# Transposed tokens of a mixture layer, laid out token by token

## The chip, the cores and the metric

One core of one Trainium2 chip runs the whole kernel. The metric is the device time of one execution in microseconds, lower is better. TensorE, VectorE, ScalarE, GpSimd and SyncE run their own instruction streams and meet at semaphores.

## What is computed

A decoder layer on 16 batches of 256 tokens by 256 numbers, in float32. Three residual blocks follow each other: a Fourier attention, a cross attention with 16 heads, and a feed-forward block of two mixture layers ("up" and "down") with 64 experts, of which each token takes two. Only the third touches the change:

```python
def kmoe(x_flat, W_router, A, B, scale, bias, d_in1, d_in2, d_out1, d_out2, top_k):
    logits = x_flat @ W_router.T
    vals, idx = jax.lax.top_k(logits, top_k)
    probs = jax.nn.softmax(vals, axis=-1)
    xs = x_flat.reshape(-1, d_in1, d_in2)
    Ag = A[idx]
    Bg = B[idx]
    Y = jnp.einsum('nkoi,nij,nkpj->nkop', Ag, xs, Bg)
    out = jnp.einsum('nkop,nk->nop', Y, probs).reshape(-1, d_out1 * d_out2)
    return out * scale + bias
x_flat = x.reshape(-1, D1 * D2)          # 64 rows of 1024 for each batch
h = kmoe(x_flat, W_up, A_up, B_up, ..., 32, 32, 64, 64, 2)
h = jax.nn.gelu(h, approximate=False)
y = kmoe(h, W_down, A_down, B_down, ..., 64, 64, 32, 32, 2)
```

A mixture token is four rows of 256, so a batch has 64 of them (`TOKENS`), each a 32 by 32 matrix.

## The kernel before

All weights lie in SBUF from the start, the activations of a batch too, and eight PSUM banks are shared by turns. The work of a batch is cut into named steps. A table of words, `ORDER`, fixes by hand in which order the steps are issued, and `step.2@1` means part 2 of the step for the batch one turn back. Every engine walks through the same table and issues those steps that it has code for, so four neighbouring batches are in flight at once and no engine ever takes its steps out of this order. A second table, `DRAIN`, orders what is left of the last two batches.

The third layer norm leaves its rows in `xn3` (128 rows by 2 by 256). The steps that then use the tensor of the change, `xn3T`, are these:

- `ln3_turn` (TensorE, L871): four transposes put `xn3` into the PSUM bank `F`, 512 columns, ordered by column half `c`, token `n` and row `r` within the token.
- `ln3_keep` (ScalarE, L674): one copy of 128 partitions by 512 numbers from `F` to `xn3T`. Before, `xn3T` is `[128, 8, 64]`: for each of the eight pairs of row `r` and half `c` the 64 tokens lie side by side.
- `logits_up` (TensorE, L882): eight matmuls, each with the 64 tokens of one `(r, c)` as the stationary operand (the weights that are loaded) and 64 columns of the router matrix `r_up` as the moving one. [...]
- `own_act` (ScalarE, L683) and `own_dve` (VectorE, L1121): eight copies each of 32 partitions by 256 numbers, from `xn3T` to `own`. Both run through `own_parts` (L362 to L367). `own` holds every token's matrix once for each of its two experts. A copy writes every fourth number there, in 32 groups (`v`, `p`) of eight (`a`), and reads for `a` a number from another of the eight rows of `xn3T`.
- `up` (TensorE, L935 and L941): the matmuls of the experts. The first part needs all of `own`, and the experts' matrices in `chosen_up`. Of those SyncE brings half by DMA (`choose_sync`, L478), 32 transfers for parts 0 to 3 and 32 for parts 4 to 7, the latter as the slots of parts 0 to 3 come free.

Around `own_dve` the table has this order, in which VectorE walks: `mask.3@1`, `own_dve@2`, `y_keep.2@3` (L1234), `catch_b.2@1` (L1087), `dn_weigh.3@3` (L1224, writes `W_dn`), `scale.3@1` (L1098), `y_keep.3@3`. On TensorE `dn_second.3@3` (L974) needs `W_dn`, and `y_turn@3` (L987) needs `y_keep.3`. Only after both does TensorE come to `up.0@2`. Around `logits_up` TensorE has `score.0@1` (L810, L813), `logits_up@2`, `q.2@1`, `q.3@1` (L797), `turn1` (L745) and `turn_a.0@1` (L820), and the last of these needs the scaled probabilities of VectorE's `scale.0@1` (L1098).

Of the kernel before, what the change touches and what calls it, by code (L numbers as in the profile page):

```python
# [16 lines left out]
P = 128  # L17
BATCH, SEQ, DIM = 16, 256, 256
RT = SEQ // P
CT = DIM // P  # L20
HEADS, KEY = 16, 64
PAIRS = HEADS // 2
EXPERTS, TOPK = 64, 2
TOKENS = SEQ * DIM // 1024
D1, F1 = 32, 64
UP_TOK = P // D1
# [23 lines left out]
def at(b, per_batch, k):  # L50

    return b * per_batch + k


def after(eng, sem, value):

    if value > 0:
        eng.wait_ge(sem, value)
# [133 lines left out]
def decoder_layer(nc, t, out):  # L192
    ctx = ExitStack()
    with ctx:
        def sb(name, shape, dt=F32):
            return ctx.enter_context(nc.sbuf_tensor(name, shape, dt))
# [26 lines left out]
        r_up = sb("r_up", [P, 2 * UP_TOK, EXPERTS])  # L223
# [13 lines left out]
        xn = sb("xn", [P, RT, DIM])  # L237
        xnT = sb("xnT", [P, CT, SEQ])
        xn3 = sb("xn3", [P, RT, DIM])
        xn3T = sb("xn3T", [P, 4 * CT, TOKENS])  # L240
        stats = sb("stats", [P, 3, RT, 6])
        moments = sb("moments", [P, 3, RT, 2])
        var_eps = sb("var_eps", [P, 3, RT])
# [20 lines left out]
        h = sb("h", [P, UP_PAIRS * UP_TOK * F1])  # L264
# [30 lines left out]
        def bank(name):  # L295
            return ctx.enter_context(nc.psum_tensor(name, [P, 512], F32))

        S0, S1, PT, X, P0, P1, F, G = (bank(n) for n in ("S0", "S1", "PT", "X", "P0", "P1", "F", "G"))
# [57 lines left out]
        def wait_f(eng, name, n, b):  # L356
            eng.wait_ge(f_kept, f_turns[name, n, b] + 1)
# [4 lines left out]
        def own_parts(n, il):  # L362

            half, k = divmod(n, TOPK)
            dst = own[n * D1:(n + 1) * D1, :].rearrange("j (v p k a i) -> j k i v p a", v=UP_PAIRS, p=UP_TOK, k=TOPK, i=4)
            src = xn3T[il * D1:(il + 1) * D1, :, :].rearrange("j a (v h p) -> j h v p a", h=2, p=UP_TOK)
            return dst[:, k, il], src[:, 1 - half]  # L367

        def share_of(name, layer, b):
# [221 lines left out]
        def _(act):  # L591
# [79 lines left out]
            def ln3_keep(c):  # L671
                act.wait_ge(xn3_turned, at(c, 1, 1))
                after(act, own_dve, at(c, 8, 0))
                act.copy(xn3T[:, :, :].rearrange("p (r c) n -> p c n r", c=CT),  # L674
                         F[:, :].rearrange("p (c n r) -> p c n r", c=CT, r=4)).then_inc(f_kept, 1)

            def spread_tokens(c):
                wait_f(act, "ln3_turn", None, c)
                act.wait_ge(zeroed, 1 + DN_SLOTS)
                after(act, first_done[0], at(c, UP_PAIRS, 0))  # L680
                for n in (0, 1):
                    for il in range(4):
                        act.copy(*own_parts(n, il)).then_inc(own_act, 1)  # L683
# [5 lines left out]
            def gelu(c):  # L689
# [9 lines left out]
                for i in range(2):  # L699
# [3 lines left out]
            run({"xnT1": lambda f: xnT_keep(f, 1), "xnT2": lambda f: xnT_keep(f, 2), "f_keep": f_keep, "k_keep": k_keep,  # L703
                 "v_keep": v_keep, "q_keep": q_keep, "power": power, "exp": exp, "catch_a": catch_a, "keep_out": keep_out,
                 "ln3_keep": ln3_keep, "own_act": spread_tokens, "gap_up": lambda c: gap_of(c, 0),
                 "gap_dn": lambda c: gap_of(c, 1), "gelu": gelu,
                 "choose_act": choosing(act, act.copy, mybir.EngineType.Activation, "act")})

        @block.tensor
        def _(pe):  # L710

            pe.wait_ge(fourier_tables, 16 * FOURIER_LOADS)
            for i, s in enumerate((S0, S1, PT)):
                for ct in range(CT):
                    for j in range(2):
                        mm = pe.matmul(s[:, ct * 256:(ct + 1) * 256], wnat[:, i, j, ct * P:(ct + 1) * P],
                                       dft[:, j, :], start=(j == 0), stop=(j == 1))
                mm.then_inc(folded, 1)
            for half in range(2):
                for j in range(2):  # L720
                    mm = pe.matmul(P0[:, 4 * half:4 * half + 3], dft[:, j, half * P:(half + 1) * P],
                                   bnat[:, j, :], start=(j == 0), stop=(j == 1))
# [139 lines left out]
            def take_g(name, n, c):  # L862
                after(pe, g_kept, g_turns[name, n, c])
# [11 lines left out]
            def logits_up(c):  # L875
                take_g("logits_up", None, c)
                wait_f(pe, "ln3_turn", None, c)
                pe.wait_ge(ffn_tables, 16 * FFN_LOADS)
                for r in range(UP_TOK):
                    for ct in range(CT):  # L880
                        n = r * CT + ct
                        mm = pe.matmul(G[0:F1, 0:EXPERTS], xn3T[:, r * CT + ct, :], r_up[:, n, :],  # L882
                                       start=(n == 0), stop=(n == 2 * UP_TOK - 1))
                mm.then_inc(logits_done[0], 1)

# [94 lines left out]
            def y_turn(c):  # L980
# [3 lines left out]
                for d in range(8):  # L984
# [6 lines left out]
            run({"turn1": lambda f: turn_xn(f, 0), "turn2": lambda f: turn_xn(f, 1), "f": f_proj, "k": k_proj, "v": v_proj,  # L991
                 "inverse": inverse, "q": q_proj, "score": score, "turn_a": turn_a, "turn_b": turn_b, "pv": pv,
                 "wo": wo_proj, "ln3_turn": ln3_turn, "logits_up": logits_up, "spread_up": lambda c: route_spreading(c, 0),
                 "up": up, "router_dn": router_dn, "logits_dn": logits_dn, "fold": fold_logits,
                 "spread_dn": lambda c: route_spreading(c, 1), "dn_first": dn_first, "dn_second": dn_second, "y_turn": y_turn})

        @block.vector
        def _(dve):
# [116 lines left out]
            def spread_tokens(c):  # L1115
                wait_f(dve, "ln3_turn", None, c)
                dve.wait_ge(zeroed, 1 + DN_SLOTS)
                after(dve, first_done[0], at(c, UP_PAIRS, 0))
                for n in (2, 3):
                    for il in range(4):  # L1120
                        dve.tensor_copy(*own_parts(n, il)).then_inc(own_dve, 1)  # L1121
# [186 lines left out]
```

## Time and profile before

| | before |
|---|---|
| median of 3 runs | 1339.0 us (1336.48 to 1341.79) |
| the profiled execution, time | 1340.02 us |
| the profiled execution, span | 1338.2 us |
| mean granted TensorE clock | 0.96 |
| TensorE busy | 1218.3 us, 91% |
| ScalarE busy | 1086.6 us, 81% |
| VectorE busy | 964.2 us, 72% |
| GpSimd busy | 595.4 us, 44% |

All rows come from one execution whose span is 1338.2 us; 1.8 us of its time lie outside the span. It lies 1.0 us above the median of the three runs. In the stretches below, "busy" is the time in which an engine had an instruction under way, and the rows of matmuls overlap each other. `PEld` are TensorE's weight loads.

### The profile page before, as it was taken

The numbers are of one execution on the slowest core, as the hardware profiler recorded it, in microseconds if no ns is written. First come the engines' busy times: TensorE is split into PE (matmuls) and PEld (weight loads), VectorE is DVE, ScalarE is ACT, GpSimd is POOL, SyncE is SP. The second block draws the span as 40 slices with busy tenths as digits, with TensorE's granted clock in tenths as the row PEclk, the third lists the DMA queues.
The fourth block names the chain that finished last, engine by engine and source line by source line (L and its number), as shares of the span: only waits on it lengthen the run. The fifth ranks groups of instructions, "written<-read, shape, count | busy, mean of one in ns | idle before, by whom it ended". The sixth has DMA issues, their size and how long they took to land.

```text
span 1338.2 us, 51821 instructions
## 1 busy us (share of the span) xinstructions
PE 1218.3 (91%) x16466; PEld 975.4 (73%) x16466; DVE 964.2 (72%) x3677; ACT 1086.6 (81%) x3158; POOL 595.4 (44%) x1846
## 2 busy tenths in 40 slices
PE   7799899999999999999999999999999999988645
PEld 5567687777778787777778777777878777765534
DVE  1465779696877869696887969597887959686634
ACT  2465899898988989898989989898889979887663
POOL 2122436363544636264544635364554626352432
PEclk9899999999999999999999999999999999998655
DMA  9200101010010101010010101001010101001000
GB/s 290 45 9 18 34 13 42 15 39 22 19 42 10 42 12 42 17 36 25 17 36 17 41 12 41 20 26 34 14 39 13 41 16 36 17 16 28 9 19 10
DMA packets 66209, 42.57 MB, mean 32 GB/s; under 512 B 18065, under 2 KB 64786, under 8 KB 65682
## 3 DMA queue, kind: packets, MB, share of 16 engines
q1 hardware_dynamic: 65938, 39.25, 10.5%
q8 instruction: 134, 2.20, 0.7%
q14 instruction: 137, 1.12, 0.3%
HBM read 34.98 MB, written 4.19 MB: 29 GB/s over the span
## 4 chain that ended last, share of the span: by engine, by line
PE 56%; DVE 16%; issue 10%; SPq 9%; ACT 3%; DMA 2%; POOL 1%; DVEq 1%; POOLq 0%; ACTq 0%
SPq L478 8%; PE P L797 5%; PE P L765 5%; PE PT L820 5%; PE X L855 4%; PE P L776 4%; PE PT L855 4%; PE P L754 3%; PE F L935 3%; PE X L842 3%; DVE own L1121 3%; PE F L960 3%; DVE chosen_dn L418 3%; PE S L813 3%; PE G L894 2%
## 5 line engine op out<-in xcount | busy, mean ns | idle before, releaser
L418 POOL COPY chosen_dn<-experts 64x64 f32 x1000 | 222.5, 279 | 219.2 <-issue 149.8
L657 ACT ACTIVATE probs<-probs,neg_max 128x128 f32<-128x128 f32 (+1 forms) x512 | 226.4, 444 | 23.6 <-DVE neg_max L1080 20.4
L404 POOL COPY chosen_up<-experts 32x128 f32 x512 | 182.8, 357 | 105.2 <-POOL chosen_up L404 51.7
L404 ACT COPY chosen_up<-experts 32x128 f32 x528 | 156.1, 296 | 17.3 <-PE G L941 4.5
L1080 DVE CUSTOM_DVE_ANT_0 probs<-S,distance 128x128 f32<-128x128 f32 (+1 forms) x512 | 151.9, 351 | 14.6 <-PE S L813 11.1
L820 PE MATMUL PT<-ident,probs 128*128 128x128 f32 x768 | 136.7, 287 | 10.6 <-DVE probs L1098 7.8
L696 ACT ACTIVATE hT<-h 64x1024 f32<-64x1024 f32 x64 | 126.7, 1980 | 8.5 <-DVE h L1211 7.1
L1098 DVE TENSOR_TENSOR probs<-probs,rinv 128x768 f32<-128x768 f32 x128 | 129.1, 1009 | 4.4
L765 PE MATMUL P<-ctxT,wk 128*128 128x256 f32 x512 | 122.3, 383 | 0.9 <-DVE x L1058 0.9
L776 PE MATMUL P<-wv,ctxT 128*128 128x256 f32 x512 | 122.5, 382 | 0.0
L820 PEld LDWEIGHTS PT<-ident,probs 128*128 128x128 f32 x768 | 86.4, 142 | 49.1 <-issue 31.5
L1087 DVE COPY probsT<-PT 128x384 f32<-128x384 f32 x128 | 71.3, 557 | 70.2 <-PE PT L820 69.0
L935 PEld LDWEIGHTS F<-chosen_up,own 64*64 64x64 f32 x2048 | 77.3, 141 | 59.4 <-issue 41.8
L935 PE MATMUL F<-chosen_up,own 64*64 64x64 f32 x2048 | 91.5, 231 | 31.2 <-DMA chosen_up<-in_experts_up 18.7
L797 PE MATMUL P<-xnT,wq 128*128 128x256 f32 x512 | 117.7, 383 | 0.8 <-ACT xnT L610 0.8
L418 ACT COPY chosen_dn<-experts 64x64 f32 x528 | 86.9, 239 | 36.0 <-issue 30.2
L521 POOL TENSOR_SCALAR var_eps<-moments 128x2 f32<-128x2 f32 x48 | 10.5, 219 | 228.0 <-DVE moments L1010 226.8
L797 PEld LDWEIGHTS P<-xnT,wq 128*128 128x128 f32 x512 | 94.7, 190 | 14.0 <-issue 1.4
L765 PEld LDWEIGHTS P<-ctxT,wk 128*128 128x128 f32 x512 | 94.9, 193 | 12.6 <-DVE x L1058 1.3
L776 PEld LDWEIGHTS P<-wv,ctxT 128*128 128x128 f32 x512 | 93.4, 190 | 11.2
L657 ACT ACTIVATION_READ_ACCUMULATOR probs<-probs,neg_max 128x1 f32 x512 | 95.8, 187 | 0.0
L941 PE MATMUL G<-chosen_up,W 64*64 64x64 f32 x2048 | 91.8, 232 | 3.6 <-DVE W L1202 2.8
(131 smaller groups left out, 2836.2 us busy)
## 6 DMA issues: line engine op xcount, KB each, us to landing
chosen_up<-in_experts_up SPq DMA_DIRECT2D x992, 16.0 KB, 1.6
x<-in_x SPq DMA_DIRECT2D x16, 256.0 KB, 2.6
ctxT<-in_ctxT SPq DMA_DIRECT2D x16, 256.0 KB, 2.8
out<-x2b SPq DMA_DIRECT2D x16, 256.0 KB, 2.2
experts<-in_experts_up SPq DMA_DIRECT2D x2, 1024.0 KB, 19.4
wk<-in_xWk SPq DMA_DIRECT2D x1, 1024.0 KB
wo<-in_xWo SPq DMA_DIRECT2D x1, 1024.0 KB
wv<-in_xWv SPq DMA_DIRECT2D x1, 1024.0 KB, 7.6
```

What stands on the lines that cost most here:

```text
L404: last = copy(to[row:row + D1, n * 2 * F1:(n + 1) * 2 * F1], experts_up[k][:, bass.ds(held[g % loaded(units), unit], 2 * F1)])
L418: last = copy(dst, src.rearrange("p (m c) -> p m c", m=2))
L478: sp.dma_start(chosen_up[v % UP_SLOTS][row:row + D1, n * 2 * F1:(n + 1) * 2 * F1], t["experts_up"][:, bass.ds(at_sp[g % loaded(units), uni ...
L657: act.activation(probs[:, e % 4, lo:hi], probs[:, e % 4, lo:hi], ACT.Exp, bias=neg_max[:, e % 4, rt:rt + 1], scale=-1.0, accum_out=rsum[:, ...
L696: act.activation(dst, src, ACT.Gelu).then_inc(hT_ready, 1)
L765: mm = pe.matmul(bank[:, i * 256:(i + 1) * 256], wk[:, ct, m * P:(m + 1) * P], ctxT[:, ct, :], start=(ct == 0), stop=(ct == CT - 1))
L776: mm = pe.matmul(bank[:, rt * 256:(rt + 1) * 256], ctxT[:, ct, rt * P:(rt + 1) * P], wv[:, ct, j * 256:(j + 1) * 256], start=(ct == 0), st ...
L797: mm = pe.matmul(bank[:, i * 256:(i + 1) * 256], wq[:, ct, m * P:(m + 1) * P], xnT[:, ct, :], start=(ct == 0), stop=(ct == CT - 1))
L820: mm = pe.transpose(PT[:, j * P:(j + 1) * P], probs[:, e % 4, j * P:(j + 1) * P], ident[:, :])
L935: mm = pe.matmul(F[rows, one], own[rows, m * F1:(m + 1) * F1], chosen_up[v % UP_SLOTS][rows, b:b + F1], start=True, stop=True)
L1080: dve.tensor_tensor_reduce(probs[:, e % 4, lo:hi], S[e % 2][:, lo:hi], distance[:, (1 - rt) * P:2 * P], SLOPES[e], TOP, ALU.add, ALU.min, ...
L1098: dve.tensor_tensor(wide, wide, by, ALU.mult).then_inc(probs_scaled, 1)
```

## The change

`xn3T` gets the shape `[128, 64, 8]`: the eight numbers of a token lie side by side, and from one token to the next it is eight floats (32 bytes). All users follow. `ln3_keep` writes the same 512 numbers, now with a step of two floats inside each half. The copies of `own_parts` read eight neighbouring numbers for each token, 32 for each group of four tokens, and write as before. `logits_up` loads its 64 stationary columns with a step of eight floats. The number and the order of the instructions are the same on every engine, and no semaphore changes.

```diff
-        xn3T = sb("xn3T", [P, 4 * CT, TOKENS])
+        xn3T = sb("xn3T", [P, TOKENS, 4 * CT])
...
             dst = own[n * D1:(n + 1) * D1, :].rearrange("j (v p k a i) -> j k i v p a", v=UP_PAIRS, p=UP_TOK, k=TOPK, i=4)
-            src = xn3T[il * D1:(il + 1) * D1, :, :].rearrange("j a (v h p) -> j h v p a", h=2, p=UP_TOK)
+            src = xn3T[il * D1:(il + 1) * D1, :, :].rearrange("j (v h p) a -> j h v p a", h=2, p=UP_TOK)
...
-                act.copy(xn3T[:, :, :].rearrange("p (r c) n -> p c n r", c=CT),
+                act.copy(xn3T[:, :, :].rearrange("p n (r c) -> p c n r", c=CT),
                          F[:, :].rearrange("p (c n r) -> p c n r", c=CT, r=4)).then_inc(f_kept, 1)
...
-                        mm = pe.matmul(G[0:F1, 0:EXPERTS], xn3T[:, r * CT + ct, :], r_up[:, n, :],
+                        mm = pe.matmul(G[0:F1, 0:EXPERTS], xn3T[:, :, r * CT + ct], r_up[:, n, :],
                                        start=(n == 0), stop=(n == 2 * UP_TOK - 1))
```

## Rows read from the trace of the kernel before

**Rows 1.** Busy time by stretch of the span: start:end, length, engines, clock
```profile
200.00:1150.00 950.00, 915.01 (x12882) 735.25 (x12881) 750.84 (x2850) 838.75 (x2448) 471.40 (x1452) 1.00 0.10 27
1210.00:1270.00 60.00, 40.93 (x624) 31.27 (x619) 35.86 (x143) 39.81 (x115) 24.05 (x85) 0.74 0.05 14
```
**Rows 2.** Waits of TensorE over the span: total us, times, longest
```profile
PE F L935 <- DMA chosen_up<-in_experts_up: 18.7, 16, 2.4
PE G L974 <- DVE W_dn L1224: 18.0, 23, 2.1
...
PE PT L820 <- DVE probs L1098: 7.8, 16, 1.9
```
**Rows 3.** The chain that ended last, 663 to 673 us: start, us, what
```profile
663.95 0.42 DVE own L1121
664.40 0.40 DVE own L1121
...
667.43 0.06 DVE experts L1234
...
668.24 0.56 DVE probsT L1087
668.83 0.69 DVE W_dn L1224
...
671.92 0.21 PE F L987
```
**Rows 4.** Timeline, 655 to 673 us: start, us, engine, line
```profile
663.95 3.45 DVE L1121 COPY own<-xn3T 32x256 f32<-32x256 f32 x8
...
666.35 5.38 ACT L683 COPY own<-xn3T 32x256 f32<-32x256 f32 x8
...
669.66 0.65 PE L974 MATMUL G<-chosen_dn,W_dn 128*32 128x64 f32 x32 [0.51 <-DVE W_dn L1224]
...
671.92 0.21 PE L987 MATMUL F<-ident,experts 32*128 32x32 f32 x1 [0.27 <-DVE experts L1234]
```
**Rows 5.** ScalarE's groups by shape: busy us, mean ns of one
```profile
L696 ACT ACTIVATE hT<-h 64x1024 f32<-64x1024 f32 x64 | 126.7, 1980 | 8.5 <-DVE h L1211 7.1
...
L683 ACT COPY own<-xn3T 32x256 f32<-32x256 f32 x128 | 83.4, 651 | 2.8
...
L669 ACT COPY attnT<-X 128x256 f32<-128x256 f32 x128 | 47.2, 369 | 37.1 <-PE X L845 36.7
L632 ACT COPY vals<-P 128x512 f32<-128x512 f32 x64 | 37.4, 584 | 6.0 <-PE P L776 5.6
L701 ACT ACTIVATE h<-h 128x1024 f32<-128x1024 f32 x32 | 32.1, 1050 | 0.5
...
L674 ACT COPY xn3T<-F 128x512 f32<-128x512 f32 x16 | 16.7, 1042 | 0.0
```
**Rows 6.** VectorE's groups by shape: busy us, mean ns of one
```profile
L1121 DVE COPY own<-xn3T 32x256 f32<-32x256 f32 x128 | 52.7, 412 | 4.0
...
L404 DVE COPY chosen_up<-experts 32x128 f32 x16 | 3.9, 243 | 0.4
...
L1000 DVE COPY h<-bv 128x1024 f32<-128x1024 f32 x1 | 0.7, 694 | 16.6 <-DMA experts<-in_xbo 16.6
```
**Rows 7.** TensorE's weight loads by shape: busy us, mean ns of one
```profile
L797 PEld LDWEIGHTS P<-xnT,wq 128*128 128x128 f32 x512 | 94.7, 190 | 14.0 <-issue 1.4
...
L882 PEld LDWEIGHTS G<-r_up,xn3T 128*64 128x64 f32 x256 | 16.9, 143 | 9.2 <-DVE pm_dn L1190 8.8 <-issue 0.4
```
**Rows 8.** TensorE's timeline, 632 to 648 us
```profile
636.53 3.64 PE L797 MATMUL P<-xnT,wq 128*128 128x256 f32 x16
640.00 0.59 PE L911 MATMUL G<-route_diag,route_ones 128*128 128x256 f32 x2
...
641.49 1.15 PE L882 MATMUL G<-r_up,xn3T 128*64 128x64 f32 x16
642.56 3.72 PE L797 MATMUL P<-xnT,wq 128*128 128x256 f32 x16
...
646.96 0.52 PE L820 MATMUL PT<-ident,probs 128*128 128x128 f32 x3 [0.24 <-DVE probs L1098]
```
**Rows 9.** ScalarE's timeline, 639 to 643 us
```profile
639.39 1.04 ACT L674 COPY xn3T<-F 128x512 f32<-128x512 f32 x1
640.22 1.02 ACT L641 ACTIVATE qT<-P,bq_scaled,q_scale 128x256 f32<-128x256 f32 x2
642.23 0.68 ACT L418 COPY chosen_dn<-experts 64x64 f32 x4 [0.98 <-issue]
```
**Rows 10.** All engines' busy time in one batch's stretches
```profile
657.90:672.60 14.70, 13.91 (x229) 11.02 (x224) 14.03 (x47) 14.31 (x42) 9.13 (x30) 1.00 0.10 28
```

## The prediction

> **What bounds the kernel now.** I read the stretches first. From 200 to 1150 us the batches repeat every 76 us or so, and TensorE is busy for 915 of 950 us at the full clock [rows 1]: 35 us of idle time are left for twelve and a half batches, 2.8 us a batch. So TensorE is nearly the bound, and what another engine saves can come back only where TensorE waits for it. The second view, TensorE's waits, tells where that is [rows 2]: for the experts' DMA (18.7 us over 16 batches), for `W_dn` of VectorE (18.0) and for VectorE's scaled probabilities (7.8). The third, the chain, joins them: in each batch that I followed it it runs down VectorE's queue through the eight spreading copies, `y_keep.2`, `catch_b.2` and the weighing that makes `W_dn`, and reaches TensorE at L987 [rows 3]. The DMA wait comes later, and its transfers start when the first parts of `up` have freed their slots, so whatever brings `up.0` forward brings them forward too; they don't take the gain back. Near the end, 1210 to 1270 us, the clock is 0.74 and TensorE idle for a third of the time [rows 1]; waits rule there.
>
> **The spreading copies.** What a stride costs here can be read from pairs of rows of like size [rows 5]. On ScalarE plain copies take 369 ns for 256 numbers and 584 for 512, which is 0.84 ns a number. The strided read of L696 takes 1980 ns against 1050 for the same 1024 numbers and function in plain order: 0.91 ns a number more. The strided write of L674 takes 1042 against 584: 0.89 more. The spreading copies stride on both sides and take 651 against 369, 1.10 more. So the two penalties mostly overlap. The change takes the stride from the read only. The write side, one number in each 16 bytes, stays. I price it by the nearest row, L674's write: 369 + 0.89 x 256 = 597 ns, 54 less than now. The bounds are 651 (the write alone rules) and 369 (a step of 16 bytes costs nothing, unlike L674's 256 bytes and more).
>
> [...]
>
> On VectorE plain copies from SBUF take 243 ns for 128 numbers and 694 for 1024 [rows 6], 0.50 a number, so 256 plain ones would take 307. The spreading copy takes 412, 105 above. If the write keeps 0.89/1.10 = 0.81 of that, it takes 392: **20 ns less each, 0.16 us for the eight of a batch**. Bounds: nothing, and 105 ns each, 0.84 us a batch.
>
> Where does it count? VectorE's eight run back to back for 3.45 us, directly ahead of `W_dn`, for which TensorE waits 0.51 us, and of `y_keep.3`, for which it waits 0.27 [rows 4]. So 0.16 us comes back in full in each batch that has this wait. I count 14 batches: 2.2 us. ScalarE's eight take 5.38 us [rows 4] and would take 0.43 less. The steps behind them, `v_keep.2` and `catch_a.3`, were not waited for by TensorE, which was at its projections until 674 us; I cost this gain at nothing. Its cover is the last projection; were that gone, up to 0.4 us a batch would count.
>
> **`ln3_keep`.** One copy a batch, 1042 ns [rows 5]. Its write step falls from 512 bytes to 8. Bounds: 584, the plain copy, and, since no row has such a small step, 1.5 times the present, about 1560. I take it unchanged, because no two neighbouring numbers are written one after the other, as now. It ends at 640.4 us, TensorE asks for the result at 641.49, and ScalarE idles for 0.98 us soon after [rows 8, 9]. Either bound is hidden: half a microsecond more would end at 640.9. What it covers is TensorE's wait for its `G` bank, which ends at the same 641.49. In the drain it starts at 1247.3 and TensorE asks at 1251.8. Zero.
>
> **The router's loads.** No row shows a strided load of weights. `logits_up` is 16 loads and 16 matmuls, from 641.49 to 642.56, when L797 starts: 67 ns a pair. L797 itself has 16 pairs in 3.47 us, 217 ns each [rows 8], though one load is recorded at 190 ns [rows 7]: loads run beside the matmuls of the pair before. The records grow by about 50 ns from 64 to 128 columns [rows 7], 0.8 ns a column, so a plain load of 64 columns has some 50 ns of work in a pair of 67. Bounds for the strided one: 50 ns again (TensorE doesn't mind), no cost; or ScalarE's penalty of 0.91 a number on top, 0.84 + 0.91 = 1.75 ns by 64 columns = 112 ns, and the pair becomes 112: 45 x 16 = 0.72 us a batch; or twice that load, 224 ns, 2.5 us a batch. Of this TensorE's wait before L820 takes the first 0.24 us [rows 8]: VectorE's probabilities, which end it, hang on `score.0`, ahead of the loads. `top_up` on VectorE is reached well after the logits are there. I take the cost as nothing seen: pairs of plain loads leave 17 ns of room, the cover another 15 ns for each (0.24/16), and TensorE's other loads keep up everywhere. It is a narrow choice, and the least sure of this text.
>
> **The sum.** 1340.0 of the profiled execution, -2.2 for VectorE's copies, 0 for ScalarE's, `ln3_keep` and the loads: 1337.8. The median of the runs shown is 1.0 below that execution, so 1336.8. That is 0.2% less, and about half a per cent, 6.7 us, is what a measurement of this kernel can tell from no change.
>
> **Rivals.**
> 1. *The loads take ScalarE's penalty.* 0.72 - 0.24 - 0.16 = +0.32 us a batch, 14 times: +4.5 us, **1343.5**. For it: two engines show nearly the same price for isolated numbers [rows 5, 6], which looks like a property of the memory. Against: TensorE's load has a path of its own, and nothing in the trace shows it. The mixed case, a load of up to 92 ns, gives back just what the copies gain (25 x 16 = 0.40 = 0.24 + 0.16), and the time stays at 1339.
>    The Trainium skill, "Advanced Engine Details and Errata", "SBUF Cachelines", speaks against the change here: a line has 16 bytes, and unless two accesses in a row fall on it there is a penalty. It names no engine. ScalarE's rows agree with it; no row shows it for TensorE. With its word taken for the loads, the time is this rival's.
> 2. *The loads become the bound of `logits_up` outright, slower than before.* From a load of 122 ns on (55 x 16 = 0.88 = 0.24 + 0.16 + 0.48) the net loss passes 0.48 us a batch, 6.7 us in all. At 224 ns it is 2.5 - 0.4 = 2.1 us a batch, 29 us: **1368**; at 150 ns, 1.33 - 0.4 = 0.93, +13 us, **1352**. For it: rival 1 is already near. Against: it needs more than ScalarE's price for a hop.
> 3. *The write step of 16 bytes is nearly free, and the read ruled.* VectorE's copies fall to 307 ns, ScalarE's to 369. VectorE would give 0.84 us a batch, but in this stretch TensorE is idle for only 14.70 - 13.91 = 0.79 us [rows 10], so 0.79 x 14 = 11 us: **1328**, with rival 1's loads about 1334. What is late next is TensorE itself. For it: the reads hop 256 bytes, the writes only 16. Against: reading and writing together cost more than reading alone, 1.10 against 0.91, so the write costs something.
> 4. *The diff doesn't shorten the copies at all* (the write alone sets 651 and 412): 1339, or rival 1's loss without the gain, 1346.
>
> **How the numbers follow.** Forecast, loads hidden and copies a little shorter: 0.40, between 1334 and 1339. Rival 1 with its mixed case: 0.25. Rival 2: 0.10. Rival 3: 0.18, of which a third with slow loads. Rival 4: 0.07. Faster by over 0.5% takes rival 3 with free loads, 0.12, part of the rest of it, 0.03, and the upper part of the forecast, where the copies give over 60 ns each, 0.09: 0.24. Slower by over 0.5%: rival 2's 0.10, and 0.06 from the edges of rivals 1 and 4: 0.16. Same: 0.60. The range leaves out rival 2 above 1346 and the lowest tenth, under 1329: 1329 to 1346.
>
> **What would show it.** In the changed profile: L1121 at 392 ns, L683 near 597, L674 at 1042; the wait for `W_dn` at L974 shorter by 0.16 us a batch; `logits_up` still 1.07 us from its first matmul to the next L797, and the wait before L820 still there. The forecast is wrong if that stretch grows beyond 1.3 us (then the loads bind and the wait before L820 is gone), or if L1121 falls under 350 ns. It is wrong in its mechanism if the copies shorten as said and the waits of TensorE at L974 and L987 do not.

## The result, and the profile after

| | before | changed |
|---|---|---|
| median | 1336.48 us (7 runs, 1333.83 to 1341.79) | 1342.48 us (7 runs, 1339.55 to 1346.32) |
| the profiled execution, time | 1340.02 us | 1346.32 us |
| its span | 1338.2 us | 1344.6 us |

The ratio is 1.0042 with a 95% interval of 1.0023 to 1.0062: 6 us slower, a small loss that is clear of the noise. More runs of the kernel before were made beside the changed one, so its median is now 2.5 us under the 1339.0 that stood ahead of the prediction. The profiled execution of the changed kernel is the slowest of its seven; it is compared below with the profiled one of before, which is 3.5 us above the median of its kernel.

TensorE's timeline of the changed kernel around the router's matmuls, which answers to [rows 8]; columns are start, us, engine, line, operation, tiles, count:

```profile
641.46 3.66 PE L797 MATMUL P<-xnT,wq 128*128 128x256 f32 x16
644.96 0.59 PE L911 MATMUL G<-route_diag,route_ones 128*128 128x256 f32 x2
...
646.44 2.14 PE L882 MATMUL G<-r_up,xn3T 128*64 128x64 f32 x16
648.51 3.72 PE L797 MATMUL P<-xnT,wq 128*128 128x256 f32 x16
...
652.50 0.49 PE L820 MATMUL PT<-ident,probs 128*128 128x128 f32 x3
```

The profile shows 16 pairs of weight load and matmul for the eight matmuls of the code. From the first of the 16 pairs to the next L797 it is 648.51 - 646.44 = 2.07 us, where it was 1.07. A pair takes 129 ns instead of 67, and it is so in each of the 15 batches that run at the full clock; the sixteenth runs at a granted clock of 0.50 before and 0.91 after, and can't be compared. The bracket behind L820 is gone: TensorE now comes to the transposes after the probabilities are ready.

What the users of the tensor cost now, from the groups by shape of the changed kernel, beside [rows 5 to 7] (mean ns of one stands behind the busy time):

```profile
L882 PEld LDWEIGHTS G<-r_up,xn3T 128*64 128x64 f32 x256 | 31.9, 216 | 9.2 <-DVE pm_dn L1190 8.8 <-issue 0.4
...
L1121 DVE COPY own<-xn3T 32x256 f32<-32x256 f32 x128 | 52.2, 408 | 4.0
...
L683 ACT COPY own<-xn3T 32x256 f32<-32x256 f32 x128 | 82.4, 644 | 2.8
...
L674 ACT COPY xn3T<-F 128x512 f32<-128x512 f32 x16 | 9.9, 617 | 0.0
```

The recorded load went from 143 to 216 ns. The spreading copies went from 412 to 408 ns and from 651 to 644, next to nothing. `ln3_keep` went from 1042 to 617, near the 584 of a plain copy of that size, and nothing came of it, as it was hidden.

TensorE's waits over the changed kernel's span, beside [rows 2]:

```profile
PE F L935 <- DMA chosen_up<-in_experts_up: 23.0, 19, 3.9
PE G L974 <- DVE W_dn L1224: 18.0, 23, 2.2
...
PE PT L820 <- DVE probs L1098: 3.1, 4, 1.9
```

The wait for the probabilities fell from 7.8 us in 16 waits to 3.1 in 4, so the cover of the loads was used up. The wait for `W_dn` is the same 18.0 us over the span; between 200 and 1150 us it went from 6.9 to 6.2 us in 13 waits, 0.05 us a wait, about what the slightly shorter copies gave. The DMA wait is 4.3 us longer, 3.4 us of that after 1150 us, where one wait takes 3.9; it moves by more between executions of other kernels here (11.8 to 19.0 us in the runs below), and I read nothing from it.

### The profile page after: what moved, and what is told of

Read it like the earlier page. It is cut to its first block, busy times and chain, and to the rows that moved or that the text cites. A ratio compares the mean times of both kernels' runs of the same rounds, so it can differ in the third digit from the quotient of the medians.

```text
span 1344.6 us, 51821 instructions
## 1 busy us (share of the span) xinstructions
PE 1225.0 (91%) x16466; PEld 987.6 (73%) x16466; DVE 962.6 (72%) x3677; ACT 1081.9 (80%) x3158; POOL 594.1 (44%) x1846
## 4 chain that ended last, share of the span: by engine, by line
PE 58%; DVE 13%; SPq 11%; issue 9%; ACT 3%; DMA 2%; POOL 1%; DVEq 1%; ACTq 0%; POOLq 0%
SPq L478 10%; PE P L797 8%; PE P L776 4%; PE X L855 4%; PE P L765 4%; PE PT L820 4%; PE PT L855 4%; DVE own L1121 3%; PE P L754 3%; PE F L935 3%; PE X L842 3%; PE F L960 3%; PE G L894 3%; PE G L882 2%; PE G L974 2%
## 5 line engine op out<-in xcount | busy, mean ns | idle before, releaser
L820 PE MATMUL PT<-ident,probs 128*128 128x128 f32 x768 | 135.8, 286 | 5.8 <-DVE probs L1098 3.1
L797 PE MATMUL P<-xnT,wq 128*128 128x256 f32 x512 | 117.7, 383 | 0.8 <-ACT xnT L610 0.8
L820 PEld LDWEIGHTS PT<-ident,probs 128*128 128x128 f32 x768 | 86.8, 142 | 41.8 <-issue 24.2
L797 PEld LDWEIGHTS P<-xnT,wq 128*128 128x128 f32 x512 | 94.9, 190 | 13.8 <-issue 1.4
```

The costliest lines, as they stand in the source:

```text
L797: mm = pe.matmul(bank[:, i * 256:(i + 1) * 256], wq[:, ct, m * P:(m + 1) * P], xnT[:, ct, :], start=(ct == 0), stop=(ct == CT - 1))
L820: mm = pe.transpose(PT[:, j * P:(j + 1) * P], probs[:, e % 4, j * P:(j + 1) * P], ident[:, :])
```

## The experiments

Each kernel's time is given against the kernel before, run on the same chip in the same session. Where there was only one execution of it, its time says little, and the durations in its profile are what counts.

**The changed layout with plain loads.** The router's loads read 64 neighbouring floats.

```diff
-                        mm = pe.matmul(G[0:F1, 0:EXPERTS], xn3T[:, :, r * CT + ct], r_up[:, n, :],
+                        mm = pe.matmul(G[0:F1, 0:EXPERTS], xn3T[:, n * 8:(n + 1) * 8, :].rearrange("p n a -> p (n a)"), r_up[:, n, :],
```

> The changed layout, but the router's loads read 64 neighbouring floats (wrong tokens for each load, as many numbers). Theory (the strided loads are the whole loss): the stretch of the 16 pairs falls from 2.07 us back to 1.07, the recorded load from 216 ns to 143, and the time is back at that of the kernel before, 1336 to 1337, since the copies gave only 4 and 7 ns each. Rival (something else of the layout costs, such as the copies or ln3_keep getting in other engines' way): the time stays above 1340.

```profile
L882 PEld LDWEIGHTS G<-r_up,xn3T 128*64 128x64 f32 x256 | 16.1, 138 | 9.2 <-DVE pm_dn L1190 8.8 <-issue 0.4
```

Measured: 1336.04 us against 1336.83, ratio 0.9983 (0.9963 to 1.0003). The stretch is 1.08 us, the load 138 ns, and the wait for the probabilities is back at 7.6 us in 16 waits. The first theory holds: with the loads plain, nothing is left of the loss.

**The kernel before with strided loads alone.**

```diff
-                        mm = pe.matmul(G[0:F1, 0:EXPERTS], xn3T[:, r * CT + ct, :], r_up[:, n, :],
+                        mm = pe.matmul(G[0:F1, 0:EXPERTS], xn3T[:, :, :].rearrange("p a n -> p (a n)").rearrange("p (b n s) -> p b s n", s=8, n=TOKENS)[:, n // 8, n % 8, :], r_up[:, n, :],
```

> The kernel before, with the router's loads alone at a step of eight floats (wrong tokens for each load). Theory: stretch of the pairs 2.07 us, wait before L820 gone, time up by 5 to 7 us as in the change, about 1342. Rival: the loss needs the whole layout, and the time stays under 1339.

```profile
644.39 2.13 PE L882 MATMUL G<-r_up,xn3T 128*64 128x64 f32 x16
646.45 3.72 PE L797 MATMUL P<-xnT,wq 128*128 128x256 f32 x16
```

Measured: 1342.94 against 1336.83, ratio 1.0073 (1.0049 to 1.0097), the stretch 2.06 us, the load 216 ns. The loads alone bring the loss. The middle of the ratio means nearly 10 us, more than the 5 to 7 expected and than the 6 of the change; the medians differ by 6.1, and the intervals of this kernel and of the change overlap. The copies are as before in it, 652 and 412 ns.

**Smaller steps of the loads**, the same edit with `s=4` and with `s=2`.

> The kernel before, router's loads at a step of four floats, 16 bytes. If what counts is that every number lies in a line of 16 bytes of its own, the pair takes 129 ns as with a step of eight (stretch 2.07 us). If the cost grows with the step, it lies between 67 and 129.

> The kernel before, router's loads at a step of two floats, 8 bytes, so two numbers in each 16. If lines of 16 bytes rule (as ln3_keep's fall from 1042 to 617 ns suggests for ScalarE), the pair stays near 67 ns and the load near 143. If every break between neighbours costs, it takes 129.

The router's loads at a step of four floats, from the groups by shape of that kernel:

```profile
L882 PEld LDWEIGHTS G<-r_up,xn3T 128*64 128x64 f32 x256 | 31.9, 215 | 9.2 <-DVE pm_dn L1190 8.8 <-issue 0.4
```

And at a step of two:

```profile
L882 PEld LDWEIGHTS G<-r_up,xn3T 128*64 128x64 f32 x256 | 17.3, 143 | 9.2 <-DVE pm_dn L1190 8.8 <-issue 0.4
```

The stretches are 2.06 us at four and 1.10 at two, against 1.07 plain; the single times were 1343.7 and 1335.0 us. So the price doesn't grow with the step. It is there in full at 16 bytes, where each number lies in 16 bytes of its own, and all but absent at 8 bytes. That is what the Trainium skill, "Advanced Engine Details and Errata", "SBUF Cachelines", states of lines of 16 bytes and two accesses to each; that TensorE's weight loads fall under it is shown by these rows.

**The kernel before with the router's matmuls issued twice.** The logits are right all the same.

```diff
-                for r in range(UP_TOK):
-                    for ct in range(CT):
...
+                for again in range(2):
+                    for r in range(UP_TOK):
+                        for ct in range(CT):
...
```

> The kernel before, with the eight router matmuls issued twice over: 16 more pairs of plain loads, 1.07 us more of TensorE's time at the same place, as much as the strided loads add. Theory (the loss is just TensorE's time there, less its cover): 5 to 7 us slower, 1342 to 1344. Rival (a strided load also disturbs others, by taking the memory): clearly less than the change, under 1340.

```profile
643.36 2.08 PE L883 MATMUL G<-r_up,xn3T 128*64 128x64 f32 x32
645.36 3.72 PE L797 MATMUL P<-xnT,wq 128*128 128x256 f32 x16
```

Measured: 1341.68 against 1336.46, ratio 1.0052 (1.0030 to 1.0075), the stretch 2.00 us. Plain work of nearly the same length in the same place costs the same within the intervals. So no contention for the memory or the like is needed to explain the loss: TensorE's time there, less the wait that covered the first part of it, is enough. This rests on the nine runs. Single executions scatter: in the profiled one the first and the last `ln3_keep` lie only 2.0 us further apart than before, with 12.9 us of DMA waits where the kernel before had 18.7. The intervals leave room for a share of a few us from something else.

**Which side of the spreading copies costs.** First the kernel before, reading with its stride but writing eight neighbours:

```diff
-            dst = own[n * D1:(n + 1) * D1, :].rearrange("j (v p k a i) -> j k i v p a", v=UP_PAIRS, p=UP_TOK, k=TOPK, i=4)
+            dst = own[n * D1:(n + 1) * D1, :].rearrange("j (v p k i a) -> j k i v p a", v=UP_PAIRS, p=UP_TOK, k=TOPK, i=4)
```

> The kernel before, with the spreading copies reading as they do (each number 256 bytes from the one before) but writing eight neighbouring numbers (the order inside own is another, so the experts get permuted tokens). If the dearer side alone rules a copy, ScalarE's stays near 640 ns and VectorE's near 400. If the write was the only costly side, they fall to 369 and 307.

```profile
L683 ACT COPY own<-xn3T 32x256 f32<-32x256 f32 x128 | 82.3, 643 | 2.8
...
L1121 DVE COPY own<-xn3T 32x256 f32<-32x256 f32 x128 | 50.8, 397 | 4.0
```

Measured: 643 ns on ScalarE, 397 on VectorE, the single time 1337.6 us. With the write plain the copies stay nearly where they were (651 and 412), just as they do with the read plain (644 and 408). Then the same edit on the changed kernel, so that neither side strides:

> The changed kernel with the same plain write, so that neither side strides (permuted tokens again). ScalarE's copy 369 ns, VectorE's 307: 0.8 us a batch on VectorE's part of the path, of which TensorE can use at most the 0.79 us it is idle there. The strided loads stay. Theory (the loss and this gain sit on the same path and add up): 1342.5 minus up to 11, so 1332 to 1336. Rival (VectorE's copies aren't on the path as read): 1342.

The copies of that kernel, from its groups by shape:

```profile
L1121 DVE COPY own<-xn3T 32x256 f32<-32x256 f32 x128 | 43.4, 339 | 4.0
...
L683 ACT COPY own<-xn3T 32x256 f32<-32x256 f32 x128 | 51.6, 403 | 2.8
```

Only now do they fall: from 644 to 403 ns and from 408 to 339. That is 34 and 32 ns above the prices I had for plain copies; whether the 32 groups of eight cost that was not tried. The time is 1334.70 us against 1336.46, ratio 0.9981 (0.9961 to 1.0002). So beside the changed kernel (1.0042) the plain write brings about 8 us, and the strided loads, still at 216 ns, take most of it. The wait for `W_dn` at L974 fell from 18.0 us in 23 waits to 11.2 in 10. The 13 waits between 200 and 1150 us are all gone, which confirms that VectorE's copies were on the path.

Last, the changed kernel with a write step of two floats:

```diff
-            dst = own[n * D1:(n + 1) * D1, :].rearrange("j (v p k a i) -> j k i v p a", v=UP_PAIRS, p=UP_TOK, k=TOPK, i=4)
+            dst = own[n * D1:(n + 1) * D1, :].rearrange("j (v p k x a i) -> j k x i v p a", v=UP_PAIRS, p=UP_TOK, k=TOPK, x=2, i=2)[:, :, il // 2]
...
-            return dst[:, k, il], src[:, 1 - half]
+            return dst[:, k, il % 2], src[:, 1 - half]
```

> The changed kernel with the copies writing every second number, a step of 8 bytes, two to a line of 16 (permuted tokens). If lines of 16 bytes rule, the copies cost nearly as e6's (about 380 and 310 ns). If any break between neighbours costs, they stay at 644 and 408.

Measured: 414 and 340 ns, against 403 and 339 with neighbours; the single time 1334.8 us. Two numbers to 16 bytes are enough for the writes of both engines too.

**A version with two numbers to every 16 bytes everywhere.** `xn3T` holds pairs of rows, so that the loads step by two floats and the copies read pairs. `own` takes its 32 rows in the order in which the copies read them, and the experts' A matrices get the same order of rows before launch.

```diff
-        xn3T = sb("xn3T", [P, 4 * CT, TOKENS])
+        xn3T = sb("xn3T", [P, 2 * CT, TOKENS, 2])
...
-            dst = own[n * D1:(n + 1) * D1, :].rearrange("j (v p k a i) -> j k i v p a", v=UP_PAIRS, p=UP_TOK, k=TOPK, i=4)
-            src = xn3T[il * D1:(il + 1) * D1, :, :].rearrange("j a (v h p) -> j h v p a", h=2, p=UP_TOK)
-            return dst[:, k, il], src[:, 1 - half]
+            dst = own[n * D1:(n + 1) * D1, :].rearrange("j (v p k i a) -> j k i v p a", v=UP_PAIRS, p=UP_TOK, k=TOPK, i=4)
+            src = xn3T[il * D1:(il + 1) * D1, :, :, :].rearrange("j a (v h p) r -> j h v p a r", h=2, p=UP_TOK)
+            return dst[:, k, il].rearrange("j v p (a r) -> j v p a r", r=2), src[:, 1 - half]
...
-                act.copy(xn3T[:, :, :].rearrange("p (r c) n -> p c n r", c=CT),
-                         F[:, :].rearrange("p (c n r) -> p c n r", c=CT, r=4)).then_inc(f_kept, 1)
+                act.copy(xn3T[:, :, :, :].rearrange("p (s c) n r -> p c n s r", c=CT),
+                         F[:, :].rearrange("p (c n s r) -> p c n s r", c=CT, s=2, r=2)).then_inc(f_kept, 1)
...
-                        mm = pe.matmul(G[0:F1, 0:EXPERTS], xn3T[:, r * CT + ct, :], r_up[:, n, :],
+                        mm = pe.matmul(G[0:F1, 0:EXPERTS], xn3T[:, r // 2 * CT + ct, :, r % 2], r_up[:, n, :],
...
+    def rows_of_own(v):
+        return v.reshape(E, F1, 2, 2, CT, 4).transpose(0, 1, 5, 2, 4, 3).reshape(E, F1, D1)
...
-        "experts_up": np.stack([a["L0_ffn_A_up"], a["L0_ffn_B_up"]], 1).transpose(3, 0, 1, 2).reshape(D1, -1),
+        "experts_up": np.stack([rows_of_own(a["L0_ffn_A_up"]), a["L0_ffn_B_up"]], 1).transpose(3, 0, 1, 2).reshape(D1, -1),
```

> A version meant to have all the plain sides. xn3T lies in pairs of rows: step of two floats from token to token for the router's loads, pairs of neighbours for the reads of the copies; own holds its 32 rows in the order in which the copies read them, so that they write eight neighbours, and the experts' A matrices get the same order of rows before launch. Theory (two numbers to each 16 bytes are enough on every engine): pair of loads 67 to 69 ns, copies 369 to 380 ns on ScalarE and 307 to 315 on VectorE, ln3_keep about 600; time e6's 1334.7 less the 0.64 us a batch of the strided loads, so 1325 to 1328. Rival (pairs of neighbours with hops between them aren't enough for the copies): copies near 600 and 400 ns, time 1336.

Its groups by shape:

```profile
L683 ACT COPY own<-xn3T 32x256 f32<-32x256 f32 x128 | 52.9, 413 | 2.8
...
L1121 DVE COPY own<-xn3T 32x256 f32<-32x256 f32 x128 | 43.2, 338 | 4.0
...
L882 PEld LDWEIGHTS G<-r_up,xn3T 128*64 128x64 f32 x256 | 17.3, 143 | 9.1 <-DVE pm_dn L1190 8.7 <-issue 0.4
...
L674 ACT COPY xn3T<-F 128x512 f32<-128x512 f32 x16 | 9.8, 615 | 0.0
```

And TensorE's waits between 200 and 1150 us of its span:

```profile
PE F L935 <- DMA chosen_up<-in_experts_up: 11.1, 12, 2.0
PE F L935 <- POOL chosen_up L404: 4.3, 3, 1.6
PE G L904 <- DVE parts L1126: 3.9, 12, 0.3
PE PT L820 <- DVE probs L1098: 3.0, 10, 0.5
```

Measured: **1327.12 us against 1337.18, ratio 0.9926 (0.9900 to 0.9951)**, faster than both kernels. All sides are cheap at once, though the copies take 413 and 338 ns and not the 369 to 380 and 307 to 315 expected, and the wait for `W_dn` is gone from this stretch. In the same stretch of the kernel before it was the second longest:

```profile
PE F L935 <- DMA chosen_up<-in_experts_up: 13.1, 13, 2.4
PE G L974 <- DVE W_dn L1224: 6.9, 13, 0.6
PE G L904 <- DVE parts L1126: 3.9, 12, 0.3
PE PT L820 <- DVE probs L1098: 3.3, 10, 0.6
```

The 6.9 us of 13 waits are what could come back there. In the profiled executions the first and the last `ln3_keep` lie 1126.3 us apart, 7.5 less than before, much the same; the medians differ by 10.1, and where the rest comes from is not shown. TensorE is nearly the bound, and this is what was to be had from a place that looked like 0.79 us a batch.

## Why the prediction was wrong

The time was forecast unchanged, with a small gain as the likeliest. It came out 0.42% slower: inside the range, and less than the half per cent that the text called measurable, but the interval lies wholly above 1, so it is a loss.

**The step that failed** is "I take the cost as nothing seen", on the router's loads. A pair took 129 ns, not 67: 1.00 us a batch. My middle bound was 112 ns from ScalarE's penalty of 0.91 ns a number. The recorded load grew by 73 ns for 64 columns, 1.14 ns each, and the pair by 62 ns, so it was somewhat dearer still; by the text's own figures it lies just past 122 ns, where rival 2 began, though the whole loss stayed under the half per cent. The reasons for zero were that TensorE's other loads keep up and that a pair has 17 ns of room. But all those loads are plain, so they say nothing of a strided one. The nearest row of a strided access to SBUF was ScalarE's, and it pointed to rival 1. I had named it and put it at 0.25. One of its reasons was read wrongly: ScalarE and VectorE don't show nearly the same price, as the spreading copy costs 1.10 ns a number above plain on ScalarE and 105/256 = 0.41 on VectorE.

**The spreading copies.** "If the write keeps 0.89/1.10 = 0.81 of that" failed as well, though little hung on it: 4 ns came back on VectorE and 7 on ScalarE, not 20 and 54, and the wait for `W_dn` shortened by 0.05 us, not 0.16. The rows of before show a strided read alone at 0.91 ns more a number, a strided write alone at 0.89, both at 1.10, from copies of other shapes. The runs on this one shape show 651 with both sides strided, 644 with the read plain, 643 with the write plain and 403 with neither. The dearer side sets the time, and removing one side of two is worth next to nothing. This is rival 4, which had 0.07.

**The combination** was in the text, as "rival 1's loss without the gain": +7 us. Measured are 6.0 from the medians. From the pair's 1.00 us, less the 0.24 of cover and the 0.07 that VectorE's eight copies gave (3.45 to 3.38 us in one batch), 0.69 a batch would be 9.7 us over 14 batches. The starts of `ln3_keep` in the first and the last batch lie 1133.8 us apart before and 1142.5 after, 8.7 more; the rest of the span gave 2.3 back. These are two single executions. With the same slow loads the distance grew by 4.1 us at a step of eight and by 8.2 at a step of four in the kernel before, and what follows the last `ln3_keep` took 85.9 to 90.9 us in the eleven executions, 90.9 in the kernel before and 89.4 in the changed one. The granted clock between 1210 and 1270 us was 0.74 before and 0.89 after, but it doesn't order them: the changed kernel with plain writes had 0.72 and took 87.1 us. So the 2.3 us lie inside what executions differ by, and the size of the loss is known from the medians alone.

**What held.** The cover in front of L820 was there and was used up. VectorE's copies were on the path: shortened by 69 ns each against the changed kernel, 8 x 0.069 x 14 = 7.7 us, they went with about 8 us (7.8 from the medians, and 7.5 from the first to the last `ln3_keep`); ScalarE's shorter copies came in the same edit and were not told apart from them. `ln3_keep` was hidden, 425 ns less of it included. My value for it, unchanged at 1042, was wrong; its lower bound of 584 was near.

## What to carry to other kernels

When a tensor is laid out anew, list every reader and writer of it and count for each how many numbers it takes from 16 neighbouring bytes: here two were enough for the writes of copies on ScalarE and VectorE, for their reads of neighbouring pairs, and for TensorE's weight loads, and one cost 20 to 70% more (VectorE's copy 408 ns against 339, `ln3_keep` on ScalarE 1042 against 617). A copy that strides on both sides gains only when both are mended. An engine that is busy 96% of the time is the wrong place to pay for savings elsewhere, and a layout of pairs can serve both sides, as it did here.

## What was not expected of the hardware

- A step of 8 bytes is nearly as cheap as none: ScalarE's copy of 512 numbers took 617 ns against 584 plain and 1042 with steps of 512 bytes; the spreading copies 414 and 340 ns against 403 and 339; the router's pair 69 ns against 67. The Trainium skill, "Vector Engine (DVE) Microarchitecture Reference", "The SBUF access granule: adjacent pairs", asks for address-adjacent pairs for the full rate. In these runs VectorE's writes of numbers that are not adjacent, but two to 16 bytes, did as well (340 ns against 339 with neighbours); the measurement decides. Reads of VectorE and ScalarE at such a step were not tried.
- TensorE's weight loads pay for a step as the other engines do, and in full from 16 bytes on: 216 ns at 32 bytes, 215 at 16, 143 at 8 and 143 plain. The pair of load and matmul grows by 62 ns, hardly less than the load's 73, so nearly all of the longer load shows where the matmul has only 64 columns.
- A read penalty and a write penalty overlap almost wholly within one copy: ScalarE's took 651 ns with both, 644 and 643 with one and 403 with neither, VectorE's 412, 408, 397 and 339.
